# Router of a mixture layer: gate folded through the output projection, half 0's routing inside the attention, queries and keys two units ahead

## The reference, cut to what matters

```python
t = t + attn(ln(t))         # 8 heads of 16, softmax over 256 tokens of an image, then @ wproj.T
x = ln(t)                   # per token: (t - mean) / sqrt(var + 1e-5)
gate_logits = x @ gate_weight.T                 # 16 experts
top_vals, top_idx = top_k(gate_logits, 2)
routing_w = softmax(top_vals)
h = silu(einsum('td,efd->tef', x, w1))          # 16 experts, 512 hidden
h_mean = sum over the tokens that chose e of h[t, e] / count[e]
y_mean = einsum('ef,edf->ed', h_mean, w2)
t = t + einsum('tk,tkd->td', routing_w, y_mean[top_idx])
```

## Time and profile before

| | us |
|---|---|
| median of 3 runs (lowest to highest) | 288.53 (283.49 to 290.47) |
| profiled execution: its time | 284.63 |
| profiled execution: its span in the trace | 282.8 |
| attention, from the first scores (157.0) to the last `unit_norm` (213.2) | 56.2 |
| from there to the first expert tile (240.7) | 27.5 |
| expert tiles and sums, to 271.3 | 30.6 |
| rest | 11.5 |

### The profile page before, as it was taken

How to read it: one execution, slowest core, us unless ns; L and a number is a source line. 1 busy time by engine, 2 the same in 40 slices (tenths; PEclk the granted TensorE clock), 3 DMA queues, 4 the chain that set the end, 5 groups by cost and what they waited for, 6 DMA issues and landing times.

```text
span 282.8 us, 7527 instructions
## 1 busy us (share of the span) xinstructions
PE 228.8 (81%) x2908; PEld 158.0 (56%) x2908; DVE 210.1 (74%) x481; ACT 177.7 (63%) x260; POOL 50.0 (18%) x64
## 2 busy tenths in 40 slices
PE   0899469999999998769999568999876605999984
PEld 0579237676767677547989456666544404233352
DVE  4757887999999999874245877888747979697512
ACT  8678979898989897058343567566673232566510
POOL 7004939800000000010002000000000277500000
PEclk9999959999999999987999999999999555799999
DMA  6920000000000000690000000000009515130002
GB/s 144 378 94 2 1 0 2 0 2 0 0 0 0 0 0 2 241 351 4 0 3 0 0 0 2 2 0 2 1 2 370 234 48 163 44 112 2 0 2 74
DMA packets 8836, 16.15 MB, mean 57 GB/s; under 512 B 752, under 2 KB 5104, under 8 KB 8432
## 3 DMA queue, kind: packets, MB, share of 16 engines
q1 hardware_dynamic: 8304, 14.83, 15.0%
q0 software_dynamic: 512, 1.05, 1.2%
HBM read 12.73 MB, written 3.15 MB: 56 GB/s over the span
## 4 chain that ended last, share of the span: by engine, by line
PE 63%; DVE 12%; ACT 9%; issue 7%; DMA 4%; POOL 2%; SPq 1%; POOLq 0%; DVEq 0%; ACTq 0%
PE ps L1275 12%; PE ps L1259 9%; PE ps L1569 8%; ACT arena L574 3%; DVE t_k L972 3%; PE ps L1342 3%; PE ps L1425 2%; PE ps L1374 2%; POOL slot_rows L490 2%; PE ps L1386 2%; PE ps L1588 2%; PE ps L1163 2%; DMA r_sb<-in_rows 2%; PE ps L1332 2%; PE ps L1398 2%
## 5 line engine op out<-in xcount | busy, mean ns | idle before, releaser
L574 ACT ACTIVATE arena<-ps,one_less_sq 128x1024 bf16<-128x1024 f32 x64 | 68.7, 1114 | 7.3 <-PE ps L1259 7.0
L1275 PEld LDWEIGHTS ps<-arena 128*128 128x128 bf16 x1536 | 47.6, 96 | 19.7 <-issue 7.4
L1275 PE MATMUL ps<-arena 128*128 (+1 forms) x1536 | 50.4, 184 | 2.2 <-ACT arena L574 2.1
L1259 PE MATMUL ps<-wide,sel 128*128 (+1 forms) x128 | 39.2, 390 | 8.1 <-ACT arena L574 6.1
L931 DVE TENSOR_REDUCE msda<-wide 128x768 f32 x32 | 45.3, 1458 | 0.0
L926 DVE TENSOR_TENSOR wide<-ps,wide 128x768 f32<-128x768 f32 x32 | 29.8, 955 | 4.0 <-PE ps L1275 4.0
L490 POOL DMA_INDIRECT slot_rows<-nrm,slots x16 | 16.5, 1034 | 72.6 <-DVE slots L1067 68.0
L1569 PE MATMUL ps<-arena,w_sb 128*32 x48 | 23.3, 632 | 0.0
L972 DVE TENSOR_REDUCE t_k<-ps 128x2 f32<-128x512 f32 x32 | 20.5, 683 | 0.0
L643 ACT ACTIVATE wide<-ps 128x512 f32<-128x512 f32 x32 | 17.3, 595 | 1.4 <-PE ps L1410 1.3
L1574 PE MATMUL ps<-late,w_sb 128*32 128x512 f32 x80 | 16.5, 662 | 0.0
(11 more groups left out here) (298 smaller groups left out, 497.3 us busy)
## 6 DMA issues: line engine op xcount, KB each, us to landing
arena<-in_w_t SPq DMA_DIRECT2D x1, 4096.0 KB, 15.0
wide<-in_w_t SPq DMA_DIRECT2D x1, 2048.0 KB, 8.0
slot_rows<-t_c SPq DMA_DIRECT2D x2, 768.0 KB, 9.9
wide<-in_w_t SPq DMA_DIRECT2D x1, 1536.0 KB, 11.3
late<-slot_rows SPq DMA_DIRECT2D x6, 256.0 KB, 3.6
w_sb<-in_weights SPq DMA_DIRECT2D x1, 1480.0 KB, 8.3
x_sb<-in_x SPq DMA_DIRECT2D x4, 128.0 KB, 2.3
wide<-in_w_t SPq DMA_DIRECT2D x1, 512.0 KB, 8.0
```

What stands on the lines that cost most here:

```text
L574: nc.scalar.activation(hot[:, u, 2 * c:2 * c + 2, :, :], ps[:, 2 * (c % 2):2 * (c % 2) + 2, :].rearrange("r p (b q) -> r p b q", b=B), ACT ...
L1259: ins = nc.tensor.matmul(ps[:, 2 * (c % 2) + p % 2, :], sel[:, bass.ds(i % 4, 1), p, :].rearrange("k h j -> k (h j)"), terms_t[:, bass.ds( ...
L1275: ins = nc.tensor.matmul(ps[:, 4 + b, p * NK * DH:(p + 1) * NK * DH], hot[:, u, p, b, :], rhs, start=(s == 0), stop=(s == PARTS - 1))
```

## The change: what it does

1. **Gate folded.** The two best experts of a token don't change when its logits are scaled, so the logits are taken from x2 without its norm. With the gate's column means taken off, logits are `std * (z1 @ gate) + o @ gate_o`, where z1 is the normalised input of the attention, o its output before the projection, and `gate_o = wproj.T @ (gate - mean)` is made once at the start (two small products on PE, a subtraction on DVE, a copy on ACT). The difference of the two best is multiplied by the reciprocal root later. The transposes and copies of `nrm` and x2 go away. x2 now enters the final sum as eight products with the identity into the output's banks.
2. **Half 0 inside the attention.** Its output is turned and projected in step 6, its residual and moments stand at the end of DVE's step 6, its logits and choice in step 7, `rank(0)` at the head of PE's step 8 and `place(0)`, `experts_of(0)` in DVE's step 8. The inverse root of half 0 is made on GpSimd from an integer guess and three Newton rounds (12 linked instructions on 128 x 4), and GpSimd normalises its four tiles. Half 1's tiles are normalised by ACT.
3. **Two units ahead.** Queries and keys of unit k + 2 are made in step k; step 0 does units 1 and 2.
4. **Staging.** ACT makes the first 6 of the 72 copies, 14 buffers instead of 16.
5. **Around it.** w2 is one load after the six reloads. The transposes of the route stand after expert groups 2 and 4. ACT makes the second half's output. `w_sb` has 128 more columns (wproj transposed).

The core of the diff:

```diff
             def unit_step(k):        # PE
+                if k == UNITS:
+                    rank(0)
                 if k < UNITS:
                     scores(k, 0)
-                if k + 1 < UNITS:
-                    project(k + 1, 0)
+                if k == UNITS - 2:
+                    turn_outputs(0)
+                if k == 0:
+                    project(1, 0)
+                elif k + 2 < UNITS:
+                    project(k + 2, 0)
                 if k >= 2:
                     weigh_values(k - 2)
                 if k >= 1 and k - 1 < UNITS:
                     scores_t(k - 1, 0)
+                if k == UNITS - 2:
+                    input_logits(0)
+                    output_logits(0)
                 if k < UNITS:
                     scores(k, 1)
                 if k >= 2:
                     turn_out(k - 2)
+                if k == UNITS - 2:
+                    project_out(0)
+                if k == UNITS:
+                    input_logits(1)
...
                 if k < UNITS:
...
                     turn_max(k)
+                if k == 0:
+                    project(2, 0)
+                    project(2, 1)
```

```diff
             def unit_step(k):        # DVE
...
-                if k + 1 < UNITS:
-                    parts(k + 1, 0)
+                if k == 0:
+                    parts(1, 0)
+                elif k + 2 < UNITS:
+                    parts(k + 2, 0)
+                if k == UNITS - 1:
+                    rank_logits(0)
+                if k == UNITS:
+                    place(0)
                 if k >= 2:
                     unit_norm(k - 2)
                 if k == UNITS:
-                    residual_stats(0)
+                    experts_of(0)
                 if k < UNITS:
                     row_max(k, 2)
                     row_max(k, 3)
+                if k == UNITS - 1:
+                    choose(0)
...
                 if k < UNITS:
                     max_rows(k)
+                if k == 0:
+                    parts(2, 0)
+                    parts(2, 1)
+                if k == UNITS - 2:
+                    residual(0)
+                    link(moments(x2_k, 0, lnf_mv))
...
+            rank_logits(1)
             choose(1)
+            residual(1)
+            moments(x2_k, 1, lnf_mv).then_inc(lnf["var"], 1)
+            place(1, rescale)
+            dve.wait_ge(lnf["norm0"], 4)
...
-            stage(range(0, GROUP))
+            stage(range(FIRST_STAGED // STAGED, GROUP))
```

```diff
+            pool.wait_ge(lnf["var"], 1)          # POOL, ahead of the scatters
+            y = root_i[:, :].bitcast(F32)
+            for n in range(3):
+                to = lnf_rstd[:, 0:4] if n == 2 else root[:, :]
+                then(nc.gpsimd.tensor_tensor(root_sq[:, :], y, y, ALU.mult))
+                then(nc.gpsimd.tensor_tensor(root_sq[:, :], root_sq[:, :], root_of[:, :], ALU.mult))
+                then(nc.gpsimd.tensor_scalar(root_sq[:, :], root_sq[:, :], -0.5, 1.5, ALU.mult, ALU.add))
+                then(nc.gpsimd.tensor_tensor(to, y, root_sq[:, :], ALU.mult))
+                y = to
+            for t in range(4):
+                nc.gpsimd.tensor_scalar(nrm[:, t, :], x2_k[:, t, :], lnf_mv[:, t, 0:1], lnf_rstd[:, t:t + 1],
+                                        ALU.subtract, ALU.mult).then_inc(lnf["norm0"], 1)
```

More of the change, by code:

```diff
@@ L48 @@
 STAGED = QUADS - 1
+FIRST_STAGED = 6
+ROUTE_AFTER = (2, 4)
+ROOT_BITS = 0x5f3759df
 EPS = 1e-5
@@ L739, in _ @@
                     columns_out(g + 2)
+                if g in ROUTE_AFTER:
+                    h = ROUTE_AFTER.index(g)
+                    act.wait_ge(rt_mm, 4 * (h + 1))
+                    nc.scalar.activation(half(route_t, h), ps[:, 7, :], ACT.Copy).then_inc(route_t_ready, 1)
+            act.wait_ge(moe_mm, 2)
+            nc.scalar.activation(half(y_out, 1), ps[:, 3, :], ACT.Copy).then_inc(y_out_ready[1], 1)
         @block.vector
@@ new lines, in choose @@
+            def choose(h):
+                tiles = slice(4 * h, 4 * h + 4)
+                for t in range(4 * h, 4 * h + 4):
+                    ins = nc.vector.max_index(top_i[:, t, :], top[:, t, :], lg[:, t, :])
+                link(ins)
+                link(nc.vector.tensor_copy(top_f[:, tiles, :], top_i[:, tiles, 0:TOPK]))
+                link(nc.vector.tensor_tensor(
+                    picked[:, :, tiles, :], expert_f[:, 0:E].unsqueeze(1).unsqueeze(1).to_broadcast([P, TOPK, 4, E]),
+                    top_f[:, tiles, :].rearrange("q t c -> q c t").unsqueeze(3).to_broadcast([P, TOPK, 4, E]), ALU.is_equal))
+                nc.vector.tensor_tensor(chosen_b[:, tiles, :], picked[:, 0, tiles, :], picked[:, 1, tiles, :],
+                                        ALU.add).then_inc(chosen_ready, 1)
@@ new lines, in place @@
+            def place(h, between=None):
+                tiles = slice(4 * h, 4 * h + 4)
+                dve.wait_ge(rank_mm, h + 1)
+                link(nc.vector.tensor_scalar(quads_e[:, h, :], ranks(h)[:, 4, :], 1.0 / GRAIN, ROUND, ALU.mult, ALU.add))
+                link(nc.vector.scalar_tensor_tensor(out=quads_before[:, :, :],
+                                                    in0=quads_e[:, h, :].unsqueeze(1).to_broadcast([P, E, E]),
+                                                    scalar=-ROUND, in1=before32[:, :, :], op0=ALU.add, op1=ALU.mult))
+                if between:
+                    between()
+                link(nc.vector.tensor_reduce(first_slot[:, h, :], quads_before[:, :, :], AX_X, ALU.add))
+                link(nc.vector.tensor_tensor(slot_of[:, :, :], ranks(h)[:, 0:4, :],
+                                             first_slot[:, h, :].unsqueeze(1).to_broadcast([P, 4, E]), ALU.add))
+                link(nc.vector.tensor_tensor(picked_slot[:, :, :, :], picked[:, :, tiles, :],
+                                             slot_of[:, :, :].unsqueeze(1).to_broadcast([P, TOPK, 4, E]), ALU.mult))
+                with nc.allow_low_precision(reason="slot numbers are whole and below 1536"):
+                    nc.vector.tensor_reduce(slots[:, :, tiles], picked_slot[:, :, :, :], AX_X, ALU.add).then_inc(slots_ready, 1)
@@ L1053, in place @@
-            def place(h):
-                tiles = slice(4 * h, 4 * h + 4)
-                dve.wait_ge(rank_mm, h + 1)
-                link(nc.vector.tensor_scalar(quads_e[:, h, :], ranks(h)[:, 4, :], 1.0 / GRAIN, ROUND, ALU.mult, ALU.add))
-                link(nc.vector.scalar_tensor_tensor(out=quads_before[:, :, :],
-                                                    in0=quads_e[:, h, :].unsqueeze(1).to_broadcast([P, E, E]),
-                                                    scalar=-ROUND, in1=before32[:, :, :], op0=ALU.add, op1=ALU.mult))
-                link(nc.vector.tensor_reduce(first_slot[:, h, :], quads_before[:, :, :], AX_X, ALU.add))
-                link(nc.vector.tensor_tensor(slot_of[:, :, :], ranks(h)[:, 0:4, :],
-                                             first_slot[:, h, :].unsqueeze(1).to_broadcast([P, 4, E]), ALU.add))
-                link(nc.vector.tensor_tensor(picked_slot[:, :, :, :], picked[:, :, tiles, :],
-                                             slot_of[:, :, :].unsqueeze(1).to_broadcast([P, TOPK, 4, E]), ALU.mult))
-                with nc.allow_low_precision(reason="slot numbers are whole and below 1536"):
-                    nc.vector.tensor_reduce(slots[:, :, tiles], picked_slot[:, :, :, :], AX_X, ALU.add).then_inc(slots_ready, 1)
@@ L1601, in _ @@
             expert_sums(SLOT_GROUPS - 1)
+            for t in range(TILES):
+                nc.tensor.matmul(tile_of(2, t), x2_k[:, t, :], ident[:, :], start=(t % 4 == 0), stop=False,
+                                 skip_group_check=True)
+            pe.wait_ge(cols_ready, SLOT_GROUPS)
             for f in range(FT):
```

307 lines of the change are left out of this document (168 added, 139 removed).

## The result

| | before | after |
|---|---|---|
| median of the runs of the first comparison | 286.41 us (4 runs) | 288.03 us (4 runs) |
| ratio after/before, 95% interval | | 1.0108 [1.0065, 1.0151] |
| the same, repeated later with 11 and 22 runs | 284.71 us | 288.16 us, 1.0104 [1.0065, 1.0143] |
| span of the profiled execution | 282.8 us | 286.2 us |
| mean granted clock of it | 0.932 | 0.915 |

The change makes the kernel 1% slower. 288.0 lies inside the predicted range, but the forecast was 285.3, a gain. By the 2% named in the prediction this is no change; the interval excludes both zero and the forecast. The ratios are of undisturbed executions alone (in some, whatever the kernel, the clock is lower and the time over 1.5% longer), so they are not quotients of the medians beside them.

A forecast was written before the change was run, and what follows sets the result against it. No single engine was taken to set the end; only 213.2 to 240.67 us could yield gains. Span 282.8 - 4.5 + 1.2 + 1.6 + 0.3 - 0.1 = 281.3, carried to 285.3 us; range 277.5 to 290.5.

The forecast's parts named there:

- What bounds the kernel: Whole kernel: no single engine sets the end; the change can gain only between 213.2 and 240.67 us.
- Steps 6 and 7: Attention: step 6 grows by 1.3 to 7.2 us through PE, step 7 by 2.1 to 7.5 through DVE.
- Steps 8 and 9: End of the attention: +1.3 us, 0.8 for `choose(0)` ahead of `max_rows(7)` and 0.5 for waiting at `rank(0)`.
- GpSimd's root: Between 206 and 214.2 us: 12 small operations and four tiles take 5.2 us together, hidden.
- Half 0's slots: Ready at 214.2 us; 15.2 us later, at 229.4 instead of 238.3, PE turns the first.
- Half 1's: Behind the attention: half 1's slots ready at 228.4 us, experts starting at 232.0 instead of 240.67.
- Staging: Expert tiles: DVE's first copy of tile 4 at 240.2 us; DVE paces groups 1 and 2, net -4.5 us.
- The rest: Start and end: route transposes +1.2 us, identity products +1.6, start +0.3, w2 nothing, ACT's half of the output -0.1.
- Attention longer still: Attention: rival with its end at the upper bound, +9.1 us; span 284.3, 0.5% slower; chance 0.07.
- Router hidden: Attention from step 6: rival using all 6.3 us of DVE's idle time; 280.6 us, 2.2% faster; chance 0.33.
- GpSimd late: POOL's queue ahead of half 0's scatters: rival, at its upper bound span 293, 3.6% slower; chance 0.10.
- Scatters locked out by copies: Half 1's eight scatters: rival, each waits for a whole DVE copy of 0.37 us; span 283.0; chance 0.05.

The follow-up runs named there:

- k_after_hot: The changed kernel with 24 idle products on PE from step 7 to around `rank(1)`, nothing else changed; 285.28 us, 0.9999 of before.
- b_two_ahead: The kernel before with queries and keys made two units ahead, nothing else; 285.92 us, 1.0043 of before.
- f_again: The changed kernel with 16 idle products on PE from step 7 to `rank(1)`, nothing else changed; 284.23 us, 0.9983 of before.
- c_move: The changed kernel with half 0's residual and moments at the end of step 7 instead of step 6; 286.33 us, 1.0038 of before.
- h_step8: The changed kernel's folded gate, but one unit ahead, half 0's router one step later and no root on GpSimd; 284.60 us, 0.9964 of before.
- m_best: h_step8 with four identity products and the route's transposes moved earlier, and each scatter waiting for its own tile only; 281.70 us, 0.9891 of before.

## Why the prediction was wrong

**What bounds the kernel** was read rightly, but not to its end. The part on the earlier trace rows noted a clock of 0.50 from 223 on as a property of the open stretch, and priced every product up to the tail by its duration at full clock. The step that failed is this unspoken one: that steps 7 to 9 keep the clock they had. The prediction's own sum held the warning. It gave DVE 7.5 us of chained work in step 7, and left PE, with 4.55 us of work in the old step, waiting for it. What the runs showed in its place: the clock fell to 0.50 at 211 us, steps 8 and 9 took 12.31 us for 9.1, half 1 came 5.5 us late, and the gain of 4.5 us forecast for the end of group 2 (250.7 for 255.2) became nothing (255.4). With the clock held that group ends at 251.3 in k_after_hot.

**Two units ahead.** -0.7 for steps 2 to 5 was forecast, -0.56 measured; `turn_max(1)` at 172.39 for 172.2. By itself the part costs 0.4% in the middle (b_two_ahead; its interval just includes nothing).

**Steps 6 and 7**: 7.62 and 7.81 us for 7.2 and 7.5. The terms were right to a few tenths. (The 0.86 us that the prediction calls PE's wait ahead of `turn_max` is that of the weight load; PE's own is 0.66.)

**Steps 8 and 9** is the term that was mis-sized: forecast 9.1 us from `turn_max(7)` to the last normalising, measured 12.3. With the clock held it is 9.0, in k_after_hot and in f_again (212.45 to 221.46). So the forecast's queueing was right, and the missing 3.3 us are the clock.

**GpSimd's root**: 12 operations of 0.20 us, 0.28 apart, and four tiles in 3.15, 6.6 us where 5.2 were forecast: the small ones 3.4 for 3.0, the tiles 3.15 for 2.2. It is hidden, as forecast. c_move shows its cover is 2.3 us thin: moved by 7.8 us, it sets the end.

**Half 0's slots**: 15.5 us from slots to PE for 15.2. **Half 1's** at 233.91 for 228.4; 229.8 in k_after_hot. **Staging**: PE waits ahead of tile 4 for DVE's copies, as forecast, but at 245.73 and not 240.2. The delay of half 1 goes straight through. In k_after_hot tile 4 starts at 241.63. DVE paces group 1 as forecast, but not group 2, where PE's pieces follow each other at 0.43 us. **The rest**: the identity products +1.6 net by forecast, and the end of the chain shows 1.98 against 0.36 of cover; the route's transposes 0.59 twice; w2 lands 14.2 us after its issue at 248.3, 13.7 ahead of its first use at 276.18.

Altogether the forecast's sum was a span of 281.3, and k_after_hot, the same kernel at held clock, has 281.4. That agreement is partly luck: the execution profiled, 283.22 us, is one of the fastest of its kernel, whose median is 285.28. Its time, 285.28 against a before of 285.09, is no gain, since the step from this span to a median was the second weak one. I carried a difference of spans, 1.5 us, from one execution of before; with the clock held in both, the medians differ by nothing.

**The rivals.** *Attention longer still* came closest: its 9.1 against 10.35 measured, though by the clock and not by late waits. *Router hidden*: no; DVE had the idle time, but not where the order put the work. h_step8 shows how much of it is to be had by another order. *GpSimd late*: not in after, seen in c_move. Its bound was added up wrongly: 206 and 28.5 us are 234.5, not 231, and every price that follows from it is too low by as much. *Scatters locked out by copies*: half 1's scatters come at 235.11, 236.37, 237.75 and 239.14, so 1.26 to 1.39 apart beside the copies, as the earlier trace rows had it. By the exclusive lock of the Trainium skill (SBUF — State Buffer, "Who interferes with whom") each would have waited for a whole copy; this trace shows a third of one at most.

**Where the 1% comes from**, as far as the runs separate it: the low clock from step 8 to `rank(1)` is 1.1 to 1.2% (after against f_again 1.2%, against k_after_hot 1.1%), which is the whole loss within the intervals. That idle products act through the clock, and not by moving something else, is shown by the durations in f_again and k_after_hot. At held clock the longer attention (48.8 us from `turn_max(0)` to the last normalising before, 55.4 in k_after_hot) is paid for by the earlier slots. What stays open: what makes the throttle let the clock fall, since it fell in c_move and h_step8 too, where PE waited less; why k_after_hot and f_again differ by more than eight products should cost, though within their intervals; and the share of the longer attention in after was not measured apart from the clock.

## What to carry to other kernels

Before work is moved into another engine's share of a tuned loop, ask what TensorE does meanwhile: if it is left waiting for half of a step, look at the granted clock of the steps behind it, and price their products at both levels. A few idle products are a cheap experiment that tells such a loss from one of queueing (8 filled step 7, 16 reached to `rank(1)`). Here they were no cure: putting the router later, where both engines had time, gave as much (h_step8), and filling its waits added nothing.

A stage that starts earlier gains only up to the next thing it needs: 7.5 us at the slots were 2.7 at the first tile, 0.8 at the fifth and nothing at the eighth. And in a tail bound by one engine, products taken out from behind it and put under an earlier wait are a gain: the three edits of m_best together gave 284.60 to 281.70 us.

## What the runs showed of the hardware that was not expected

The clock fell although PE's longest wait in step 7 was 2.5 us: PE was busy 3.82 of 7.81 us at a granted 0.95, and then ran at 0.50, 1.2 GHz, while it was busy for 9.60 of the next 12.31. The kernel before ran the same two steps at 1.00, busy for 5.63 of 7.83. It fell in h_step8 too, about 211, where PE was busy 5.34 of the 6 us ahead, and in c_move; there it was back at 1.00 within 4 us. At the lower level the sixteen weighing products take 1.94 us for 1.07, four transposes 1.11 for 0.66, the eight logit products 1.89 for 1.07.

GpSimd's operation on 128x4 elements takes 0.20 us and follows its predecessor 0.28 apart when each waits for the last, far below anything in the earlier trace rows.
